# Statistics for eight node steps at a time, an output moved from ACT to DVE in every fourth step, and GpSimd joining four steps later

## What is computed

```python
edge_msg = relu(edge_attr @ W1e + b1e) @ W2e + b2e
messages = (x[src] + edge_msg) * edge_weight[:, None]     # weight from the degrees
agg = segment_sum(messages, dst, num_segments=n)
combined = (1.0 + gin_eps) * x + agg
h = relu(combined @ W1n + b1n) @ W2n + b2n
out = h + x
out = out * rsqrt(mean(out * out, axis=-1) + RMS_EPS) * rms_w
result = layernorm(x + out)                               # mean and variance of each row
```

## Time and profile before

| | us |
|---|---|
| median of 3 runs (1272.25 to 1275.76) | 1274.73 |
| the profiled execution's own time | 1275.69 |
| its span in the trace | 1273.9 |
| busy in the span: DVE, ACT, PE, POOL | 1215.2, 1148.9, 1104.9, 998.1 |
| mean granted TensorE clock | 0.985 |

### The profile page before, as it was taken

The page is one execution under the profiler, slowest core; times in us unless marked ns, Lnnn a source line. Parts: engine busy times, 40 slices in busy tenths (PEclk is TensorE's granted clock), DMA queues, the critical chain, the costliest instruction groups (busy, mean ns, idle before and its releaser), DMA issues. The chain is left out here.

```text
span 1273.9 us, 31103 instructions
## 1 busy us (share of the span) xinstructions
PE 1104.9 (87%) x7488; PEld 826.9 (65%) x7600; DVE 1215.2 (95%) x4672; ACT 1148.9 (90%) x3932; POOL 998.1 (78%) x1302
## 2 busy tenths in 40 slices
PE   6898998999989999997988888788887889899992
PEld 3353567777777777775766666566565666677771
DVE  8999978999999999995999999999999999999998
ACT  7686958888989898986899999999999999999997
POOL 7787777777777777577777776777777777999997
PEclk9999999999999999998999999999999999999997
DMA  4799997666565566787668888877888776777654
GB/s 110 264 382 347 393 381 267 183 180 186 185 179 184 175 180 183 229 317 277 245 218 304 300 322 294 301 293 272 314 277 307 291 257 217 277 265 273 268 220 193
DMA packets 87739, 328.37 MB, mean 258 GB/s; under 512 B 24920, under 2 KB 28164, under 8 KB 63120
## 3 DMA queue, kind: packets, MB, share of 16 engines
q1 hardware_dynamic: 55848, 255.49, 54.4%
q0 software_dynamic: 30016, 69.49, 17.6%
q10 hardware_dynamic: 1704, 1.59, 0.4%
HBM read 180.18 MB, written 153.95 MB: 262 GB/s over the span
## 5 line engine op out<-in xcount | busy, mean ns | idle before, releaser
L743 POOL DMA_INDIRECT xs<-in_x,src_x x392 | 402.3, 1026 | 119.4 <-issue 118.1
L769 POOL DMA_INDIRECT agg_scratch<-staged,sca_i x384 | 381.0, 992 | 124.5 <-issue 114.9
L1670 PE MATMUL bank<-cT,w1n 128*128 128x512 f32 x392 | 214.3, 629 | 70.2 <-ACT cT L972 70.2
L1648 PEld LDWEIGHTS bank<-w2n,hn 128*128 128x128 f32 x1568 | 206.8, 193 | 70.6 <-issue 64.7
L990 ACT ACTIVATE squares<-res 128x128 f32<-128x128 f32 x784 | 247.6, 387 | 0.2 <-DVE res L1433 0.2
L1648 PE MATMUL bank<-w2n,hn 128*128 128x128 f32 x1568 | 207.7, 276 | 3.9 <-ACT hn L977 0.4
L1001 ACT ACTIVATE on<-z,offset,rstd 128x128 f32<-128x128 f32 x438 | 204.5, 566 | 0.5 <-DVE offset L1399 0.4
L990 ACT ACTIVATION_READ_ACCUMULATOR squares<-res 128x1 f32 x784 | 203.3, 281 | 0.0
L1567 PE MATMUL bank<-digits,picks 128*128 128x221 f16 x1568 | 186.1, 261 | 2.2 <-DVE digits L1307 2.2
L1319 DVE SCALAR_TENSOR_TENSOR picked<-iota_x,src_top,bank 128x221 f16<-128x221 f16 x392 | 171.1, 438 | 3.6 <-PE bank L1567 3.5
L1459 DVE BATCH_NORM_STATS2 stats<-z 128x6 f32<-128x128 f32 x784 | 168.8, 275 | 0.0
(11 more groups left out here) (190 smaller groups left out, 2156.1 us busy)
## 6 DMA issues: line engine op xcount, KB each, us to landing
agg_scratch<-zeros SPq DMA_DIRECT2D x48, 1024.0 KB
xn<-in_x SPq DMA_DIRECT2D x48, 1024.0 KB
out<-on SPq DMA_DIRECT2D x48, 1024.0 KB, 4.6
ag<-agg_scratch SPq DMA_DIRECT2D x47, 1024.0 KB, 6.7
staged<-sums_scratch POOLq DMA_DIRECT2D x28, 896.0 KB, 8.5
sums_scratch<-sums SPq DMA_DIRECT2D x47, 512.0 KB
highq<-src_key_scratch SPq DMA_DIRECT2D x49, 256.0 KB, 3.7
ea<-in_edge_attr SPq DMA_DIRECT2D x45, 256.0 KB
```

The lines of the kernel that those rows point to most:

```text
L743: pool.indirect_dma_start(out=xs[:, b % XS, j, :], out_offset=None, in_=x, in_offset=bass.IndirectOffsetOnAxis(ap=src_x[:, t:t + 1], axis= ...
L769: pool.indirect_dma_start(out=agg_rows, out_offset=bass.IndirectOffsetOnAxis(ap=sca_i[:, t:t + 1], axis=0), in_=staged[:, k % STAGES, j, : ...
L1648: last = pe.matmul(ps[4 + s][:, j * P:(j + 1) * P], hn[:, s, j * P:(j + 1) * P], w2n[:, :], start=False, stop=j == TB - 1)
L1670: pe.matmul(ps[2 + s][:, :], w1n[:, :], cT[:, s, :], start=True, stop=True).then_inc(hn_done, 1)
```

## The change

1. **Pairs of blocks.** For blocks 0 to 43 the statistics chain runs once for two blocks, on 128x32 elements: `apart`, `within`, `mean`, `between`, `neg_mean` and `total` in DVE's step 8K + 16 for pair K, `variance` in 17, ACT's `spread` in 18, `rstd` in 19, `offset` in 20. Blocks 44 to 48 keep the old chains. `stats` grows from 2 to 4 blocks.
2. **Output lags.** DVE's and POOL's outputs move from lag 18 to 20, ACT's from 20 to 21.
3. **Shares.** While POOL is away, ACT makes 3, 3, 3 and 2 outputs in the four steps of a block (`act_share`), and DVE 1, 1, 1 and 2.
4. **POOL's part** begins at m = 136 (`xsc`) and m = 120 (outputs), four steps later each.
5. **Loop.** The last loop ends after block 43 (step 175) and not at step 191; the steps behind it are written out.

The core of the diff:

```diff
-    MIX_ALONE, END_ALONE = 132, 116
+    PAIRED = (BLOCKS - 4) // 2 * 2
+    MIX_ALONE, END_ALONE = 136, 120
-        stats = sb("stats", [P, 2, BN, 6])
+        stats = sb("stats", [P, 4, BN, 6])
 def run_nodes(eng, step, tail, alone_too=True):
-            rounds = STEPS // unroll
-            first = min(MIX_ALONE + 6, END_ALONE + 16) // unroll
-            then = -(-max(MIX_ALONE + 7, END_ALONE + 20) // unroll)
+            rounds = PAIRED * SPB // unroll
+            first = min(MIX_ALONE + 6, END_ALONE + 18) // unroll
+            then = -(-max(MIX_ALONE + 8, END_ALONE + 22) // unroll)
+        def paired(n, u, lag):
+            K = (n - lag) // (2 * SPB)
+            return u % (2 * SPB) == lag % (2 * SPB) and (not isinstance(K, int) or 0 <= K < PAIRED // 2)
+        def act_share(w):
+            return TB - 2 if w % SPB == SPB - 1 else TB - 1
 POOL
-                for m, w in scaled_steps(n, u, 18, 15):
+                for m, w in scaled_steps(n, u, 20, 15):
 ACT
+                if paired(n, u, 18):
+                    K = (n - 18) // (2 * SPB)
+                    act.wait_ge(variance_ready, at(K * 2 + 2))
+                    need(act, rstd_ready, K * 2)
+                    act.activation(spread[:, :, :].rearrange("p b i -> p (b i)"), variance[:, :, :].rearrange("p b i -> p (b i)"),
+                                   ACT.Sqrt, bias=ln_eps[:, 0:1], scale=1.0 / D).then_inc(spread_ready, 2)
-                for m, w in scaled_steps(n, u, 20, 16):
+                for m, w in scaled_steps(n, u, 21, 16):
-                    share = 3 if ended_alone(m) else 1 if ...
+                    share = act_share(w) if ended_alone(m) else 1 if ...
 DVE
+                if paired(n, u, 16):
+                    K, v = (n - 16) // (2 * SPB), pair_slots(u, 16)
+                    both = stats[:, v:v + 2, :, :]
+                    dve.wait_ge(stats_ready, at((K + 1) * 2 * SPB))
+                    dve.tensor_tensor(apart2[:, :, :], both[:, :, :, 1], both[:, :, :, 4], ALU.subtract)
+                    dve.tensor_tensor(within[:, :, :], both[:, :, :, 2], both[:, :, :, 5], ALU.add)
+                    dve.tensor_tensor(mean2[:, :, :], both[:, :, :, 1], both[:, :, :, 4], ALU.add
+                                      ).then_inc(parts_ready, 2)
...
-                m, v = n - 18, (u - 18) % ZR
+                m, v = n - 20, (u - 20) % ZR
                 if live(m, STEPS) and ended_alone(m):
-                    dve.tensor_scalar(on[:, o, h, :], z[:, v, 0, :], neg_mean[:, v // SPB, h:h + 1],
-                                      rstd[:, v // SPB, h:h + 1], ALU.add, ALU.mult).then_inc(fin_ready, 1)
+                    for j in range(TB - act_share(v)):
+                        last = dve.tensor_scalar(on[:, o, h + j, :], z[:, v, j, :], neg_mean[:, v // SPB, h + j:h + j + 1],
+                                                 rstd[:, v // SPB, h + j:h + j + 1], ALU.add, ALU.mult)
+                    last.then_inc(fin_ready, 1)
```

More of the change, by code:

```diff
@@ L479, in ended_alone, with pair_slots, single @@
             return below(m, END_ALONE)
+        def paired(n, u, lag):
+            K = (n - lag) // (2 * SPB)
+            return u % (2 * SPB) == lag % (2 * SPB) and (not isinstance(K, int) or 0 <= K < PAIRED // 2)
+        def pair_slots(u, lag):
+            return (u - lag) // (2 * SPB) % 2 * 2
+        def single(k):
+            return isinstance(k, int) and PAIRED <= k < BLOCKS and not late(k)
+        def act_share(w):
+            return TB - 2 if w % SPB == SPB - 1 else TB - 1
         def late(B):
@@ L978, in node_step @@
                 k, c = (n - 16) // SPB, ((u - 16) // SPB) % 4
-                if u % SPB == 0 and live(k, BLOCKS) and not late(k):
+                if u % SPB == 0 and single(k):
                     root_variance(k, c)
+                if paired(n, u, 18):
[4 more added lines that the diff above has]
+                                   ACT.Sqrt, bias=ln_eps[:, 0:1], scale=1.0 / D).then_inc(spread_ready, 2)
                 k, c = (n - 14) // SPB, ((u - 14) // SPB) % 4
@@ L992, in node_step @@
                     last.then_inc(ssq_ready, 1)
-                for m, w in scaled_steps(n, u, 20, 16):
+                for m, w in scaled_steps(n, u, 21, 16):
                     v, B, o, h = w % ZR, m // SPB, (w // SPB) % OR, (w % SPB) * TB
-                    share = 3 if ended_alone(m) else 1 if not isinstance(B, int) or B < SPLIT else 2 if B < BLOCKS - 2 else 1 if B < BLOCKS - 1 else 2 if m < STEPS - 1 else 0
+                    share = act_share(w) if ended_alone(m) else 1 if not isinstance(B, int) or B < SPLIT else 2 if B < BLOCKS - 2 else 1 if B < BLOCKS - 1 else 2 if m < STEPS - 1 else 0
                     act.wait_ge(offset_ready, at(B + 1))
@@ L1422, in chain @@
                 k, c = (n - lag) // SPB, ((u - lag) // SPB) % 4
-                if u % SPB == phase and live(k, BLOCKS) and late(k) == of_late:
+                if u % SPB == phase and (single(k) or late(k) and k < BLOCKS) and late(k) == of_late:
                     operation(k, c)
@@ L1438, in node_step @@
                 chain(n, u, 15, 3, True, set_offset)
-                k, c = (n - 12) // SPB, ((u - 12) // SPB) % 2
-                if u % SPB == 0 and live(k, BLOCKS):
+                k, c, v = (n - 12) // SPB, ((u - 12) // SPB) % 2, ((u - 12) // SPB) % 4
+                if u % SPB == 0 and (single(k) or late(k) and k < BLOCKS):
                     dve.wait_ge(stats_ready, at((k + 1) * SPB))
-                    dve.tensor_tensor(apart2[:, c, :], stats[:, c, :, 1], stats[:, c, :, 4], ALU.subtract)
-                    dve.tensor_tensor(within[:, c, :], stats[:, c, :, 2], stats[:, c, :, 5], ALU.add)
-                    dve.tensor_tensor(mean2[:, c, :], stats[:, c, :, 1], stats[:, c, :, 4], ALU.add
+                    dve.tensor_tensor(apart2[:, c, :], stats[:, v, :, 1], stats[:, v, :, 4], ALU.subtract)
+                    dve.tensor_tensor(within[:, c, :], stats[:, v, :, 2], stats[:, v, :, 5], ALU.add)
+                    dve.tensor_tensor(mean2[:, c, :], stats[:, v, :, 1], stats[:, v, :, 4], ALU.add
                                       ).then_inc(parts_ready, 1)
+                if paired(n, u, 16):
[6 more added lines that the diff above has]
+                                      ).then_inc(parts_ready, 2)
+                if paired(n, u, 20):
+                    K, v = (n - 20) // (2 * SPB), pair_slots(u, 20)
+                    dve.wait_ge(rstd_ready, at(K * 2 + 2))
+                    dve.tensor_tensor(offset[:, v:v + 2, :], neg_mean[:, v:v + 2, :], rstd[:, v:v + 2, :], ALU.mult
+                                      ).then_inc(offset_ready, 2)
                 m, s = n - 7, (u - 7) % RR
@@ L1456, in node_step @@
                     dve.wait_ge(z_ready, at(m + 1))
-                    need(dve, parts_ready, m // SPB - 1)
+                    need(dve, parts_ready, m // SPB - 3)
                     for j in range(TB):
-                        last = dve.bn_stats(stats[:, (v // SPB) % 2, (v % SPB) * TB + j, :], z[:, v, j, :])
+                        last = dve.bn_stats(stats[:, (v // SPB) % 4, (v % SPB) * TB + j, :], z[:, v, j, :])
                     last.then_inc(stats_ready, 1)
@@ L1464, in node_step @@
                 chain(n, u, 15, 3, False, set_variance)
+                if paired(n, u, 16):
+                    K, v = (n - 16) // (2 * SPB), pair_slots(u, 16)
+                    dve.wait_ge(parts_ready, at(K * 2 + 2))
+                    dve.scalar_tensor_tensor(between[:, :, :], apart2[:, :, :], 32.0, apart2[:, :, :],
+                                             ALU.mult, ALU.mult).then_inc(between_ready, 2)
+                    need(dve, fin_ready, (K * 2 - 2) * SPB)
+                    dve.tensor_scalar(neg_mean[:, v:v + 2, :], mean2[:, :, :], -0.5, None, ALU.mult
+                                      ).then_inc(mean_ready, 2)
+                if paired(n, u, 17):
+                    K, v = (n - 17) // (2 * SPB), pair_slots(u, 17)
+                    dve.wait_ge(total_ready, at(K * 2 + 2))
+                    need(dve, spread_ready, K * 2)
+                    dve.scalar_tensor_tensor(variance[:, :, :], ssq[:, v:v + 2, :], LN_EPS, total[:, :, :],
+                                             ALU.mult, ALU.add).then_inc(variance_ready, 2)
+                if paired(n, u, 19):
+                    K, v = (n - 19) // (2 * SPB), pair_slots(u, 19)
+                    dve.wait_ge(spread_ready, at(K * 2 + 2))
+                    need(dve, fin_last, (K * 2 - 2) * SPB)
+                    dve.reciprocal(rstd[:, v:v + 2, :], spread[:, :, :]).then_inc(rstd_ready, 2)
                 k, c = (n - 17) // SPB, ((u - 17) // SPB) % 4
-                if u % SPB == 1 and live(k, BLOCKS) and not late(k):
+                if u % SPB == 1 and single(k):
                     invert_spread(k, c)
@@ L1470, in node_step @@
                 k, c = (n - 18) // SPB, ((u - 18) // SPB) % 4
```

(8 more changed lines are left out.)

## The result

| | before | after |
|---|---|---|
| median, us (lowest to highest, runs) | 1275.73 (1272.25 to 1277.47, 7) | 1267.12 (1263.38 to 1270.37, 7) |
| profiled execution, us; its span | 1275.69; 1273.9 | 1265.17; 1263.4 |
| first `res` of the node stage | 595.9 | 596.9 |
| from there to the end | 678.0 | 666.5 |
| last `res` to the end | 21.3 | 23.6 |

The ratio is 0.9933, 95% interval 0.9912 to 0.9954: faster by 0.7%. In a second series the changed kernel's median was 1265.31, ratio 0.9929 (0.9911 to 0.9947). The spans differ by 10.5 us. The table splits that: from the first `res` on, the node stage, it is 11.5 us shorter; the edge stage, which the change doesn't touch, was 1.0 longer. Over all profiled executions here the first `res` lies between 591.6 and 597.1, so a kernel's spans differ by some us before any node work.

A forecast was written before the change was run, and what follows sets the result against it. ACT was taken to bound the part without POOL, PE by a hair the part with it. Gain -15.1, plus junction 1.4, boundaries 1.0 and end 0.3, gave -12.4 us: median 1262.3, range 1259 to 1269.4.

The forecast's parts named there:

- ACT's block, 13.96: Part without POOL's help: ACT needs 13.96 us per block, 0.50 less than 14.46, and stays the bound.
- DVE's block, 13.80: Part without POOL's help: DVE needs 13.80 us per block (13.69 to 14.08), with a pair's chain taken at 1.00.
- DVE becomes the bound: Rival, part without POOL: DVE's block costs up to 14.08, gain only -7.9, or -5.3 with the junction's 4.0; chance 0.19.
- The loop boundaries, +1.0: Steps 64, 80, 96, 112: the 6.8 us loss stays and grows by 1.0 (0 to 2.0) from DVE's 2.19 stops.
- POOL's time as given: POOL's scatters set its time: free at 1075.94 whatever DVE and ACT do.
- The junction, +1.4: Where POOL joins: of the 4.0 us lost there before, 1.4 remain, since POOL is 2.6 sooner (bounds 0 and 4.0).
- the time of step 141: ACT's step 141, like step 136 before, begins at 1071.8, 3.2 us later than that step's 1068.63.
- PE sets the pace with POOL's help, zero: With POOL's help: ACT and DVE save 0.1 and 0.3 us per block, but PE sets the pace, gain zero.
- The end, 0.3: Program's end: outputs one or two steps later run into steps without squares, costing 0.3 us.
- The loads: Loads behind SP's store, one step later, stay hidden, barely; rival: `xn` comes late, slower, 1281 at 0.45 us per block; chance 0.05.
- The blocked bunch: Rival with POOL's help: POOL delays DVE's bunched small operations, gain only -3.4, 1271.3; chance 0.08 shared with "The junction eats it".
- The junction eats it: Rival where POOL joins: shorter alone steps only wait for POOL, time stays 1274.7; chance 0.08 shared with "The blocked bunch".

The follow-up runs named there:

- the kernel without pairs: Changed kernel with one statistics chain per block and the old lags, shares and POOL at 136 and 120 kept: 1272.91 us, ratio 0.9983 to the kernel before.
- The last experiment: All node steps written out, POOL at 140 and 124, plus 2-and-2 output sharing from block 44 and catching up two steps sooner: 1256.60 us, ratio 0.9859.
- 48 to 127 written, 140/124: Changed kernel with steps 48 to 127 written out instead of looped and POOL joining at steps 140 and 124: 1257.82 us, ratio 0.9867 to the kernel before.
- all written, 136/120: Changed kernel with all node steps written out and POOL still joining at steps 136 and 120: 1270.24 us, ratio 0.9962 to the kernel before.
- 132/116: Changed kernel with POOL's part moved back to steps 132 and 116, as in the kernel before: 1277.63 us, ratio 1.0024.
- the join at 140/124: Changed kernel with all node steps written out and POOL's part at steps 140 and 124, four later still: 1257.03 us, ratio 0.9867 to the kernel before.
- the one with 3 outputs: Changed kernel with ACT making three outputs in every step and POOL at 132 and 116, pairs and lags kept: 1274.04 us, ratio 0.9995.

## Why the prediction was right, and where not

Predicted 1262.3 (1258.5 to 1269.5), measured 1267.12: inside, on the dear side. Against the profiled execution the sum said -12.4, the node stage gave -11.5, and the edge stage took 1.0 of it by chance. The second profiled execution of the changed kernel, span 1258.8, had its first `res` 5.0 sooner than the first (591.9), and a node stage of 666.9. So of the 4.8 us between forecast and median, 0.9 lies in the terms and 1.0 in the median of before, which came out 1.0 higher than the one that I subtracted from. The other 2.9 can't be placed, since only profiled executions show their stages; the edge stage, whose spread of over 5 us I had not put into the range, is large enough for it. A wait for POOL in some of the executions would be too, but no profile of this kernel shows one.

- **ACT's block, 13.96.** 27.97 a pair against 27.93. Right; `on` on ACT x416.
- **DVE's block, 13.80.** The chain of a pair is 1.11, from 742.05 above and its sister rows, 0.1 over the term; DVE's block becomes about 13.86, still under ACT's 13.98. So "DVE becomes the bound" didn't occur. Its 14.08 showed in the kernel without pairs.
- **The loop boundaries, +1.0.** The four cost 7.2 instead of 6.8, +0.4, less than taken. The mechanism was another, though: I had DVE's stop as the price, and it is ACT's own stop, which stood in the trace of before (5.65 of the 6.7 there) and which I hadn't looked for.
- **POOL's time as given.** Free at 1076.80, not 1075.94, and the first `res` was as much later. Counted from the first `res`, POOL's last scatter (`joined`) began at 479.0 before, and at 478.8 and 479.5 in the two profiles of the changed kernel: for this change the term held. As a rule, "whatever DVE and ACT do" isn't shown. The other kernels with loops have 475.5 to 482.0, the six with steps 48 to 127 or all steps written out 482.2 to 487.9. Whether that is the faster alone part, the written-out code or chance stays open.
- **The junction, +1.4, and the time of step 141.** 1073.11 against 1071.8: 1.0 of it is the later first `res`, 0.4 the boundaries. ACT's step 151 ends at 1108.60 less a step (2.8) and the semaphore (0.3), 1105.5, which is 32.4 after step 141; eleven steps are 31.3, so the junction cost 1.1. The gain there, 1118.2 - 1105.5 = 12.7, is -15.1 + 1.4 + 1.0 to the tenth, but by luck: 1.1, 0.4 and the 1.0 of the edge stage stand in their place.
- **PE sets the pace with POOL's help, zero.** PE's 11.37 stands. ACT's cheaper chain let it run ahead: its `rms` stood 0.20 before PE's next transposes at 1100 and 0.96 before them at 1190; then ACT's pair is 22.73 too. That brought ACT's stores 0.7 us over nine blocks, and nothing to the end: the last `res` came 12.8 sooner and POOL's last `xsc` 12.6, as against 12.7 at step 151. Zero was right.
- **The end, 0.3.** This is the term that was mis-sized: 2.3. I let the later outputs run into steps without squares, which is so for ACT. POOL has its 4 outputs more behind its last `xsc`, and nothing frees it. The last experiment made the bunch x16 again by the lag and got 1.2 us of it back.
- **The loads.** PE waited for `xn` once, 0.6 us, in each profile of the changed kernel; when `xn` lands no view of the profile gives. The slower rival is out for this kernel, by a small margin: in the kernels written out it waited for `xn` one to five times, for up to 1.88 us (48 to 127 written, 140/124) and 1.90 (all written, 136/120), and in these two a block of the alone part took 14.72 and 14.63 instead of 14.09.
- **The blocked bunch.** `apart` was late once, by 1.5 us; in the steady blocks the bunch's `apart`, `within` and `mean` take 0.50 from start to start where they took 0.38, and PE's pace covers it.
- **The junction eats it.** Not with 136/120 in the changed kernel, and wholly with 132/116. With 136/120 and the boundaries gone it did again. The prediction's ground against it (POOL's part begins 14.0 us later) was the right one.

Where a bigger gain was to be had, the prediction didn't look: it took the 6.8 us at the boundaries as a thing that stays. Written out, and with the join at 140/124, they gave another 8 to 10 us on top of the change, 1257.03 against 1267.12 and 1265.31 (ratios 0.9867 against 0.9933 and 0.9929).

## What to carry to other kernels

When two phases meet at a time that a third party sets, shorten the first phase and move the meeting together: here each alone was worth next to nothing (0.9984 for the later meeting; 1.0024 and 0.9996 for a shorter phase with the meeting too early for it) and both 0.7 to 1.3%. Put the meeting on the late side: the extra steps cost 2.7 us per block for certain, a meeting too early cost waits of 10.5 to 13.8 us here. When a period has rare long blocks, look for the stop of the engine that is dense, and not of the one whose stop is easiest to see. An engine's slack can be worth more than the time per block says, where its own stops would otherwise be paid. And a lag that grows by steps comes back at the program's end as a bunch on the engine that finishes last.

## What the runs showed of the hardware

- Where the loop of the alone part goes round (steps 64, 80, 96, 112), ACT stops for 0.8 to 3.1 us, and DVE, in the kernels without pairs, for 1.5 to 4.4, with the releaser "issue". The period grows by the stop of the dense engine: 7.2 us for four with ACT dense in the changed kernel, 14.4 with DVE dense. With these steps written out there is none. Entering or leaving a loop shows none either. Why ACT's stop is 1.8 in the changed kernel and 2.9 in the one with 3 outputs, and what the sequencer does in it, the traces don't show.
- DVE's small operations took 0.09 to 0.13 us from start to start with 32 columns and 0.07 to 0.10 with 16: nearly all is fixed. The reciprocal took 0.26 and 0.16.
- DVE operations with two SBUF inputs came late shortly after POOL's first `xsc`, `apart` by 1.5 us in the changed kernel and by 1.05 in its second profile, and by 0.0 to 0.15 us in its steady blocks.
- After a wait of PE for 2.5 us its granted clock read 0.73 in a window of 5 us, and after one of 9.15 us 0.84 and 0.83 in two windows of 10 us, and 1.00 behind them.
- The time from the first `res` to POOL's last scatter lies between 475.5 and 487.9 us in these fourteen profiles, although POOL's work up to there is the same.
